# A state space layer's output scaling moved from VectorE to GpSimd, with two GpSimd operations written otherwise

## The chip, the cores and the metric

The kernel runs on one core of one Trainium2 chip, in one launch. The time is device microseconds of that core, from the first to the last instruction of a run; three runs were timed before the change. TensorE is called PE here, VectorE DVE, ScalarE ACT, GpSimd POOL and the sync engine, which issues the DMAs, SP.

## The reference, cut to what matters

A stack of eight layers works on x of shape (4, 32, 128, 128). The change touches one of them, the state space layer (`_mamba`), which runs over the 32 time steps of each of 4 x 128 sequences and whose result is normalised and added to x:

```python
xz = xt @ in_proj;  xc, z = xz[..., :D_INNER], xz[..., D_INNER:]
xc = silu(conv_b + sum_k conv_w[:, k] * shifted xc)        # D_INNER 256, 4 taps
dbc = xc @ x_proj
dt = softplus(dbc[..., :DT_RANK] @ dt_w + dt_b)
Bm, Cm = dbc[..., 8:24], dbc[..., 24:]                      # 16 states
dA = exp(dt[..., None] * A);  dBx = (dt * xc)[..., None] * Bm
hnew = dA_t * hprev + dBx_t;  y_t = einsum('bds,bs->bd', hnew, C_t)
y = (y + Dp * xc) * silu(z);  return y @ out_w + out_b
```

What follows the layer is h + that, then layernorm (x - mean) * rsqrt(var + 1e-5) * gain + shift, then + x.

## The kernel before

The layer is the function `mamba`. It works in 32 turns. One turn is 16 nodes of one batch entry with their 32 time steps: 512 tokens as columns (N), the 256 inner channels as two halves h of 128 partitions. A turn is cut into 16 units u. Each engine has its own program, written as a loop over slots `w` with `k, u = divmod(w, U)`; what it does in a slot, for which turn (k - 1, k, k + 1, k + 2, k + 3), is written out by `if u == ...` lines. So the engines' orders are fixed, and four turns are in flight. Semaphores alone hold the engines together; each engine takes its instructions strictly in order.

The loop of one turn k, as far as the prediction goes into it:

- PE: `project_x(k+2, h)` (L912) at u = 0 and 2 makes the channels, `flip` (L1018) turns two states' scan results every unit, `sums` (L1031) contracts them with C every second unit, `inputs` (L1004) makes the scan's input for the next two units, `project_out(k-1)` (L991) runs at u = 8.
- ACT: `x_in` (L1096) copies the channels into `xcp` at u = 0 and 2; `silu_x` (L1105) takes both convolved halves at u = 8, then `logarithms` (L1144), and in every unit `states_in` (L1170) copies the flipped states out of PSUM, which frees the bank for PE's next flip. The decays dA (L1162) of the next turn's first half run at u = 9 to 15, those of the second half at u = 0 to 4.
- POOL: `convolve(k+2, 0)` and `convolve(k+2, 1)` (L777, L779, L780: seven passes over 128 x 512 each) at u = 1 and 4. Between them stand `spread_c(k, 2)` (L816) and `gate(k-1, .)` (L823). `plus` (L788, L790) makes 1 + e at u = 15 and 0, `spread_b` (L808), `time_steps`, `bias` and `finish` (L838 to L840, gain, shift and + x) fill the rest; `deviations` (L832) gives rstd at u = 14.
- DVE: one scan (L1246, 128 x 1024) per unit, a copy of flipped states (L1256) every second unit, and at u = 5 and 7 `lost` (L1263, two inputs in SBUF), at u = 9, 11, 13 and 15 `residual`, `statistics`, `moments` and `scale(k-1)` (L1296).

A scan in the first unit of a turn waits for all 16 decays of its half, as `scan` says:

```python
dve.wait_ge(b_done, w // 2 + 1)
dve.wait_ge(dA_ready, (2 * i + h + 1) * S)
```

and the second silu of a turn waits for the second convolution, by `act.wait_ge(conv_ready, 2 * (i - EARLY) + h + 1)`.

The first turns' convolutions (0 and 1) are made on DVE ahead of the loop, so POOL convolves in turns k = 0 to 29.

Of the kernel before, what the change touches and what calls it, by code (L numbers as in the profile page):

```python
# [16 lines left out]
ALU = mybir.AluOpType  # L17
# [3 lines left out]
P = 128  # L21
B, T, W, C = 4, 32, 128, 128
# [581 lines left out]
def mamba(nc, h0, x, in_proj, conv_w, conv_b, x_proj, dt_w, dt_b, A_log, Dp, out_w, out_b, gain, shift,  # L604
# [7 lines left out]
    G, J = 4, 4  # L612
    NQ = W // Q
    N = Q * T
# [9 lines left out]
    S4 = S // 4  # L624
    with ExitStack() as ctx:
        s = Scope(nc, ctx, tag)
# [10 lines left out]
        ident = s.sb("ident", [P, P])  # L637
        m32 = s.sb("m32", [P, T])
        half_c = s.sb("half", [P, G])
        ht, hr, xt = (s.sb(n, [P, 2, G, C]) for n in ("ht", "hr", "xt"))  # L640
        hT = s.sb("hT", [P, N])
        xcp = s.sb("xcp", [P, HV, Q, PADT])
# [4 lines left out]
        e, ln = (s.sb(n, [P, HV, N]) for n in ("e", "ln"))  # L647
        bt, ct = s.sb("bt", [P, 2, G, S]), s.sb("ct", [P, 2, G, S])
        cp = s.sb("cp", [P, 2, J, G, S4])
        DB = s.sb("DB", [P, G, S, T])  # L650
        WC = s.sb("WC", [P, J, G, S4, T])
# [6 lines left out]
        z, out = s.sb("z", [P, G, C]), s.sb("out", [P, G, C])  # L658
        st, mv = s.sb("st", [P, G, 6]), s.sb("mv", [P, G, 2])
        ve, rstd = s.sb("ve", [P, G]), s.sb("rstd", [P, G])  # L660
# [25 lines left out]
        def turn(i):  # L686
            return 0 <= i < TURNS

        def unit(w):
            return 0 <= w < TURNS * U  # L690
# [62 lines left out]
        def _(pool):  # L753
            step = Chain(pool, pch)
            fill_identity(pool, step, ident)
            step(pool.memset(half_c[:, :], -0.5))
            step(pool.memset(xcp[:, :, :, 0:K - 1], 0.0))
            step(pool.memset(dA[:, :, :, :, 0:1], 0.0))
            step(pool.memset(m32[:, :], 0.0))
# [23 lines left out]
            def plus(i, h):  # L783
                pool.wait_ge(dt_read, 2 * i + h + 1)
                pool.wait_ge(e_ready, 2 * i + h + 1)
                if i >= 1:
                    pool.wait_ge(dt_ready, 2 * (i - 1) + h + 1)
                pool.tensor_tensor(dt[:, i % 2, h, :], dt[:, i % 2, h, :], e[:, h, :], ALU.add  # L788
                                   ).then_inc(plus_ready, 1)
                pool.tensor_scalar(ln[:, h, :], e[:, h, :], 1.0, None, ALU.add).then_inc(e1_ready, 1)  # L790

            def time_steps(i, h):
                pool.wait_ge(rest_ready, 2 * i + h + 1)
# [17 lines left out]
            def spread_c(i, g):  # L811
                pool.wait_ge(cp_ready, i + 1)
                if i >= 1:
                    pool.wait_ge(y_done, (i - 1) * V + G + g + 1)
                for j in range(J):
                    last = pool.tensor_tensor(  # L816
                        WC[:, j, g, :, :], cp[:, i % 2, j, g, :].unsqueeze(2).broadcast_to([P, S4, T]),
                        m32[:, :].unsqueeze(1).broadcast_to([P, S4, T]), ALU.mult)
                last.then_inc(WC_ready, 1)

            def gate(i, h):
                pool.wait_ge(y_taken, 2 * i + h + 1)
# [7 lines left out]
            def deviations(i):  # L830
                pool.wait_ge(ve_ready, i + 1)
                pool.tensor_tensor(rstd[:, :], ve[:, :], half_c[:, :], ALU.pow).then_inc(rstd_ready, 1)  # L832

            def finish(i):
                pool.wait_ge(scaled, i + 1)
# [6 lines left out]
            for w in SLOTS:  # L842
                k, u = divmod(w, U)
                if u == 0 and turn(k + 1):
                    plus(k + 1, 1)
                if u == 1:
                    if turn(k + 2) and k + 2 >= EARLY:
                        convolve(k + 2, 0)
                    if turn(k):
                        spread_c(k, 2)  # L850
                if u == 4:
                    if turn(k - 1):
                        gate(k - 1, 0)
                        gate(k - 1, 1)
                    if turn(k + 2) and k + 2 >= EARLY:
                        convolve(k + 2, 1)
                if u == 7:
                    if turn(k):
                        spread_c(k, 3)
                    if turn(k - 1):  # L860
                        bias(k - 1)
                if u in (9, 11, 13, 15) and turn(k + 1):
                    spread_b(k + 1, (u - 9) // 2)
                if u == 9 and turn(k + 1):
                    time_steps(k + 1, 0)
                    time_steps(k + 1, 1)
                if u == 11 and turn(k - 2):
                    finish(k - 2)
                if u == 14:
                    if turn(k + 1):  # L870
                        spread_c(k + 1, 0)
                    if turn(k - 1):
                        deviations(k - 1)
                if u == 15:
                    if turn(k + 2):
                        plus(k + 2, 0)
                    if turn(k + 1):
                        spread_c(k + 1, 1)
# [342 lines left out]
        def _(dve):  # L1221
            step = Chain(dve, dch)
            TT, TS, STT = dve.tensor_tensor, dve.tensor_scalar, dve.scalar_tensor_tensor
# [49 lines left out]
            def residual(i):  # L1273
                dve.wait_ge(outed, i + 1)
                dve.wait_ge(hr_ready, i + 1)
                TT(z[:, :, :], hr[:, i % 2, :, :], ps_0[:, :].rearrange("p (g c) -> p g c", g=G), ALU.add
                   ).then_inc(z_ready, 1)

# [5 lines left out]
            def moments(i):  # L1284
# [2 lines left out]
                    step.mark(dve.bn_aggr(mv[:, g, :], st[:, g, :]))  # L1287
                step.join()
                TS(ve[:, :], mv[:, :, 1], eps, None, ALU.add).then_inc(ve_ready, 1)

            def scale(i):
                dve.wait_ge(rstd_ready, i + 1)
                if i >= 1:
                    dve.wait_ge(stored, 16 * J * i)
                for g in range(G):
                    last = TS(out[:, g, :], z[:, g, :], mv[:, g, 0:1], rstd[:, g:g + 1],  # L1296
                              ALU.subtract, ALU.mult)
                last.then_inc(scaled, 1)

            for w in SLOTS:  # L1300
                k, u = divmod(w, U)
                if unit(w):
                    scan(w)
                if u % 2 == 1 and unit(w - 1):
                    states_in(w - 1)
                if u == 1 and turn(k - 1):
                    take_y(k - 1, 0)
                if k == -2 and u in (2, 4):
                    convolve(0, u // 2 - 1)
                if k == -2 and u in (10, 12):  # L1310
                    convolve(1, u // 2 - 5)
                if u == 3 and turn(k - 1):
                    take_y(k - 1, 1)
                if u in (5, 7) and turn(k + 1):
                    lost(k + 1, (u - 5) // 2)
                if u == 9 and turn(k - 1):
                    residual(k - 1)
                if u == 11 and turn(k - 1):
                    statistics(k - 1)
                if u == 13 and turn(k - 1):  # L1320
                    moments(k - 1)
                if u == 15 and turn(k - 1):
                    scale(k - 1)

# [3163 lines left out]
```

## Time and profile before

| what | value |
|---|---|
| median of three runs | 3863.41 us (3857.32 to 3867.41) |
| span of the profiled execution | 3864.4 us |
| busy share of the span: PE, DVE, ACT, POOL | 82%, 77%, 67%, 62% |
| largest group on DVE: L1246, the scan | 1141.5 us in 512 |
| L1296, the scaling on DVE | 128 instructions, median 332 ns |
| L816, the spread of C on POOL | 194.6 us in 512 |
| L790, 1 + e on POOL | 96.0 us in 64 |
| starts of the convolutions on POOL (L777), first and last | 497.6 and 1973.2 us |

The time of a run is that of the program on the core; the span of the profiled execution is the only time that the profile gives of it, and it stands 1.0 us above the median of the three runs. Read the shares with care: they are means over eight layers. The state space layer lies between about 440 and 2123 us, and the rows further down are taken from inside it. In a timeline row the first number is the start, the second how long the merged piece took, x4 means four instructions merged, and what stands in brackets is how long the engine was idle before it and what it waited for. Gaps of less than about 0.15 us are not shown as idle.

### The profile page before, as it was taken

To read this page: it belongs to the slowest core of one execution; us is meant where nothing else is said; L and a number is where in the kernel's file an instruction comes from. 1 tells how busy PE (TensorE), PEld (TensorE's weight loads), DVE (VectorE), ACT (ScalarE), POOL (GpSimd) and SP (SyncE) were. 2 spreads that over 40 slices of the span, in tenths; PEclk is the share of its full clock that TensorE was granted. 3 is DMA by queue.
4 is the path that set the end of the run, shared out by engine and by line. 5 is a ranking of instruction groups with operands and counts; after the bars stand their busy time and mean duration, and the time that the engine had idled before them with its cause. 6 is when DMAs were issued, how large, how long until landed. Compare 5 with 4: busy or idle time off the path is not lost. (4 is left out here: it accounts for less than half of the span.)

```text
span 3864.4 us, 82478 instructions
## 1 busy us (share of the span) xinstructions
PE 3158.9 (82%) x29152; PEld 2183.1 (56%) x29152; DVE 2993.7 (77%) x5896; ACT 2599.8 (67%) x5235; POOL 2377.3 (62%) x2879
## 2 busy tenths in 40 slices
PE   7999589999999999999986876688848856678486
PEld 3766356666666666666664563366636533456455
DVE  3999579999999999999997567389858663278754
ACT  4888489999999999999984210266756363077562
POOL 2899588898898999988874000177755130044850
PEclk7999799999999999999999568677769867789698
DMA  3000100000000000000000512501000014500424
GB/s 93 24 24 26 51 4 13 24 24 24 24 24 24 24 22 17 20 24 24 23 18 23 145 40 93 207 23 29 7 5 1 1 25 142 189 5 1 121 56 126
DMA packets 271007, 172.53 MB, mean 45 GB/s; under 512 B 41648, under 2 KB 249977, under 8 KB 268537
## 3 DMA queue, kind: packets, MB, share of 16 engines
q1 hardware_dynamic: 270600, 167.25, 15.1%
q8 instruction: 239, 3.92, 0.4%
q14 instruction: 168, 1.37, 0.1%
HBM read 116.59 MB, written 50.60 MB: 43 GB/s over the span
## 5 line engine op out<-in xcount | busy, mean ns | idle before, releaser
L1246 DVE TENSOR_TENSOR_SCAN mam_hs<-mam_dA,mam_ps_b 128x1024 f32<-128x1024 f32 x512 | 1141.5, 2270 | 80.9 <-issue 44.0
L1162 ACT ACTIVATE mam_dA<-mam_dt,mam_A 128x496 f32<-128x496 f32 x1024 | 658.7, 710 | 0.4
L1018 PE MATMUL mam_ps_h<-mam_ident,mam_hs 128*128 128x128 f32 x4096 | 549.6, 277 | 61.2 <-ACT mam_hTb L1170 30.8
L1018 PEld LDWEIGHTS mam_ps_h<-mam_ident,mam_hs 128*128 128x128 f32 x4096 | 454.0, 142 | 226.9 <-issue 149.2
L1170 ACT COPY mam_hTb<-mam_ps_h 128x512 f32<-128x512 f32 x768 | 424.5, 589 | 95.9 <-PE mam_ps_h L1018 95.9
L1004 PE MATMUL mam_ps_b<-mam_DB,mam_dtxt 32*128 32x512 f32 x2048 | 292.5, 638 | 77.6 <-DVE mam_hs L1246 73.6
L1031 PEld LDWEIGHTS mam_ps_y<-mam_hTb,mam_WC 128*32 128x32 f32 x8192 | 208.9, 109 | 133.2 <-issue 124.3
L1031 PE MATMUL mam_ps_y<-mam_hTb,mam_WC 128*32 128x128 f32 x8192 | 276.7, 275 | 0.3 <-issue 0.3
L780 POOL TENSOR_TENSOR mam_cv<-mam_cv,mam_tap 128x512 f32<-128x512 f32 x180 | 239.1, 1328 | 14.1
L816 POOL TENSOR_TENSOR mam_WC<-mam_cp,mam_m 128x128 f32<-128x128 f32 x512 | 194.6, 411 | 19.9 <-POOL mam_cv L780 14.8
L1256 DVE COPY mam_hTb<-mam_ps_h 128x512 f32<-128x512 f32 x256 | 174.3, 681 | 37.9 <-PE mam_ps_h L1018 35.9
L779 POOL TENSOR_TENSOR mam_tap<-mam_xcp,mam_cw 128x512 f32<-128x512 f32 x180 | 190.0, 1055 | 14.1
L460 ACT ACTIVATE gat_ex<-gat_ps_s,gat_neg 128x128 f32<-128x128 f32 x512 | 154.5, 436 | 50.6 <-DVE gat_neg L543 50.6
L2411 POOL TENSOR_TENSOR l1t_rs<-l1t_va,l1t_half 128x8 f32<-128x8 f32 x64 | 108.2, 1691 | 79.7 <-DVE l1t_va L2717 79.6
L1004 PEld LDWEIGHTS mam_ps_b<-mam_DB,mam_dtxt 32*128 32x128 f32 x2048 | 84.8, 183 | 127.9 <-issue 127.9
L256 POOL TENSOR_TENSOR gat_ex<-gat_ex,gat_den 128x512 f32<-128x512 f32 x128 | 133.0, 1050 | 36.3 <-DVE gat_den L552 36.3
L808 POOL TENSOR_TENSOR mam_DB<-mam_bt,mam_m 128x512 f32<-128x512 f32 x128 | 134.2, 1049 | 17.8 <-PE mam_ps_b L1004 17.8
L945 PE MATMUL mam_ps<-mam_xs,mam_wdt 128*128 128x512 f32 x248 | 118.4, 600 | 1.9 <-issue 1.9
L3744 POOL MEMSET sma_half<- 128x4 f32 x1 | 0.1, 103 | 184.5 <-POOLq L82 184.5
L788 POOL TENSOR_TENSOR mam_dt<-mam_dt,mam_e 128x512 f32<-128x512 f32 x64 | 81.8, 1279 | 43.3 <-ACT mam_e L1139 26.8
L543 DVE TENSOR_REDUCE gat_neg<-gat_ps_s 128x4 f32<-128x512 f32 x128 | 81.6, 679 | 22.2 <-PE gat_ps_s L343 22.2
L790 POOL TENSOR_SCALAR mam_ln<-mam_e 128x512 f32<-128x512 f32 x64 | 96.0, 1501 | 0.0
(738 smaller groups left out, 8290.4 us busy)
## 6 DMA issues: line engine op xcount, KB each, us to landing
moe_wg<-in_L_ffn_weight SPq DMA_DIRECT2D x32, 1024.0 KB, 8.2
rnn_xr<-x SPq DMA_DIRECT2D x23, 512.0 KB, 5.7
l1y_wh<-mode_weights SPq DMA_DIRECT2D x16, 544.0 KB, 3.7
gat_hg<-in_x SPq DMA_DIRECT2D x16, 512.0 KB, 7.1
h<-gat_out SPq DMA_DIRECT2D x32, 256.0 KB, 2.3
mam_ht<-h SPq DMA_DIRECT2D x128, 64.0 KB, 2.0
mam_hr<-h SPq DMA_DIRECT2D x128, 64.0 KB, 2.0
mam_xt<-in_x SPq DMA_DIRECT2D x128, 64.0 KB, 2.0
```

What stands on the lines that cost most here:

```text
L460: last = act.activation(ex[:, i % 2, h, r, :], ps_s[h][:, r * W:(r + 1) * W], ACT.Exp, bias=neg[:, i % 2, h, r:r + 1])
L779: step(pool.tensor_tensor(tap[:, :, :], xcp[:, h, :, k:k + T], weight(k), ALU.mult))
L780: step(pool.tensor_tensor(acc, acc, tap[:, :, :], ALU.add))
L808: pool.tensor_tensor(DB[:, g, :, :], bt[:, i % 2, g, :].unsqueeze(2).broadcast_to([P, S, T]), m32[:, :].unsqueeze(1).broadcast_to([P, S, T ...
L816: last = pool.tensor_tensor(WC[:, j, g, :, :], cp[:, i % 2, j, g, :].unsqueeze(2).broadcast_to([P, S4, T]), m32[:, :].unsqueeze(1).broadca ...
L1004: last = pe.matmul(ps_b[:, j, :], steps[r, g * P:(g + 1) * P], DB[r, g, :, :].rearrange("p s t -> p (s t)"), start=True, stop=True, tile_p ...
L1018: last = pe.transpose(ps_h[n][:, q * P:(q + 1) * P], hs[:, w % 3, c:c + P], ident[:, :])
L1031: last = pe.matmul(ps_y[j * T:(j + 1) * T, g * P:(g + 1) * P], WC[:, j, g, q, :], hTb[:, gg % 2, j, q, :], start=(q == 0), stop=(q == S4 - 1),
L1162: act.activation(dA[:, h, :, n, 1:], dt[:, i % 2, h, :].rearrange("p (q t) -> p q t", q=Q)[:, :, 1:], ACT.Exp, scale=A[:, h, n:n + 1]).the ...
L1170: act.copy(hTb[:, gg % 2, j, :, :], ps_h[n][:, :].rearrange("p (q d) -> p q d", q=S4)).then_inc(hB_ready if n else hA_ready, 1)
L1246: dve.tensor_tensor_scan(hs[:, w % 3, :], dA[:, h, first:first + 2, :, :].rearrange("p q s t -> p (q s t)"), ps_b[:, 2 * (w % 2):2 * (w % ...
L1256: dve.tensor_copy(hTb[:, gg % 2, 2 * (w % 2) + 1, :, :], ps_h[1][:, :].rearrange("p (q d) -> p q d", q=S4)).then_inc(hB_ready, 1)
```

## The change

Three things change, all in `mamba`. First, `scale` leaves DVE (u = 15 of the turn that follows) and is done on POOL at u = 3 of the turn after that, between `spread_c(k, 2)` and `gate(k-1, 0)`; `residual` on DVE, which writes z anew, now waits until the previous turn's z was scaled. Second, `spread_c` writes the four blocks j of a group in one instruction of 128 x 4 x 128 in place of four of 128 x 128. Third, 1 + e is a tensor_tensor with a column of ones, broadcast, in place of a tensor_scalar with the constant 1.

```diff
+        one_c = s.sb("one", [P, 1])
...
             step(pool.memset(half_c[:, :], -0.5))
+            step(pool.memset(one_c[:, :], 1.0))
...
-                pool.tensor_scalar(ln[:, h, :], e[:, h, :], 1.0, None, ALU.add).then_inc(e1_ready, 1)
+                pool.tensor_tensor(ln[:, h, :], e[:, h, :], one_c[:, :].broadcast_to([P, N]), ALU.add
+                                   ).then_inc(e1_ready, 1)
...
-                for j in range(J):
-                    last = pool.tensor_tensor(
-                        WC[:, j, g, :, :], cp[:, i % 2, j, g, :].unsqueeze(2).broadcast_to([P, S4, T]),
-                        m32[:, :].unsqueeze(1).broadcast_to([P, S4, T]), ALU.mult)
-                last.then_inc(WC_ready, 1)
+                every = [P, J, S4, T]
+                pool.tensor_tensor(WC[:, :, g, :, :], cp[:, i % 2, :, g, :].unsqueeze(3).broadcast_to(every),
+                                   m32[:, :].unsqueeze(1).unsqueeze(1).broadcast_to(every), ALU.mult).then_inc(WC_ready, 1)
...
+            def scale(i):
+                pool.wait_ge(rstd_ready, i + 1)
+                if i >= 1:
+                    pool.wait_ge(stored, 16 * J * i)
+                for g in range(G):
+                    last = pool.tensor_scalar(out[:, g, :], z[:, g, :], mv[:, g, 0:1], rstd[:, g:g + 1],
+                                              ALU.subtract, ALU.mult)
+                last.then_inc(scaled, 1)
...
+                if u == 3 and turn(k - 2):
+                    scale(k - 2)
...
             def residual(i):
                 dve.wait_ge(outed, i + 1)
                 dve.wait_ge(hr_ready, i + 1)
+                if i >= 1:
+                    dve.wait_ge(scaled, i)
...
-            def scale(i):
-                dve.wait_ge(rstd_ready, i + 1)
-                if i >= 1:
-                    dve.wait_ge(stored, 16 * J * i)
-                for g in range(G):
-                    last = TS(out[:, g, :], z[:, g, :], mv[:, g, 0:1], rstd[:, g:g + 1],
-                              ALU.subtract, ALU.mult)
-                last.then_inc(scaled, 1)
...
-                if u == 15 and turn(k - 1):
-                    scale(k - 1)
```

POOL's order in the middle of a turn, from the last two passes of the first convolution (names: cv and tap are the convolution's sum and product, WC the spread C, y the gated output). Before:

```order
L779 TENSOR_TENSOR mam_tap<-mam_xcp,mam_cw 128x512
L780 TENSOR_TENSOR mam_cv<-mam_cv,mam_tap 128x512
L816 TENSOR_TENSOR mam_WC<-mam_cp,mam_m 128x128 x4
L823 TENSOR_TENSOR mam_y<-mam_y,mam_sz 128x512 x2
L777 TENSOR_TENSOR mam_cv<-mam_xcp,mam_cw 128x512
```

and of the change:

```order
L781 TENSOR_TENSOR mam_tap<-mam_xcp,mam_cw 128x512
L782 TENSOR_TENSOR mam_cv<-mam_cv,mam_tap 128x512
L819 TENSOR_TENSOR mam_WC<-mam_cp,mam_m 128x4x128
L840 TENSOR_SCALAR mam_out<-mam_z,mam_mv,mam_rstd 128x128 x4
L824 TENSOR_TENSOR mam_y<-mam_y,mam_sz 128x512 x2
L779 TENSOR_TENSOR mam_cv<-mam_xcp,mam_cw 128x512
```

The four scalings now stand between the two convolutions; the lines are numbered two or more higher.

DVE's order at the end of a turn (hs is the scan's result, mv and ve mean and variance; the scan is printed as SCALAR_TENSOR_TENSOR here). Before:

```order
L1289 TENSOR_SCALAR mam_ve<-mam_mv 128x4
L1246 SCALAR_TENSOR_TENSOR mam_hs<-mam_dA,mam_ps_b 128x1024 x2
L1256 COPY mam_hTb<-mam_ps_h 128x512
L1296 TENSOR_SCALAR mam_out<-mam_z,mam_mv,mam_rstd 128x128 x4
L1246 SCALAR_TENSOR_TENSOR mam_hs<-mam_dA,mam_ps_b 128x1024 x2
```

and of the change:

```order
L1303 TENSOR_SCALAR mam_ve<-mam_mv 128x4
L1258 SCALAR_TENSOR_TENSOR mam_hs<-mam_dA,mam_ps_b 128x1024 x2
L1268 COPY mam_hTb<-mam_ps_h 128x512
L1258 SCALAR_TENSOR_TENSOR mam_hs<-mam_dA,mam_ps_b 128x1024 x2
```

The four scalings ahead of the next turn's first scan are gone. PE, ACT and SP keep their orders.

## Rows read from the trace of the kernel before

**Rows 1.** Stretches, 608 to 2000 us: busy us (x instructions) of PE, PEld, DVE, ACT, POOL; clock, DMA.

```profile
608.00:2000.00 1392.00, 1281.09 (x15148) 875.08 (x15148) 1311.44 (x1160) 1279.00 (x2234) 1254.28 (x1354) 1.00 0.09 22
```

**Rows 2.** Timeline of DVE, a turn's boundary: start us, us, instruction, [idle before <-releaser].

```profile
1249.23 1.19 DVE L1296 TENSOR_SCALAR mam_out<-mam_z,mam_mv,mam_rstd 128x128 f32<-128x128 f32 x4
1251.91 4.46 DVE L1246 TENSOR_TENSOR_SCAN mam_hs<-mam_dA,mam_ps_b 128x1024 f32<-128x1024 f32 x2 [1.49 <-issue]
```

**Rows 3.** Timeline of ACT, the same boundary.

```profile
1250.49 1.33 ACT L1162 ACTIVATE mam_dA<-mam_dt,mam_A 128x496 f32<-128x496 f32 x2
```

**Rows 4.** Timeline of ACT, the silu of two halves, in three turns.

```profile
519.10 1.33 ACT L1105 ACTIVATE mam_xs<-mam_cv,mam_cb 128x512 f32<-128x512 f32 x2
...
1203.18 0.59 ACT L1096 COPY mam_xcp<-mam_ps 128x512 f32<-128x512 f32 x1 [0.30 <-PE mam_ps L912]
...
1224.73 1.41 ACT L1105 ACTIVATE mam_xs<-mam_cv,mam_cb 128x512 f32<-128x512 f32 x2
...
1228.51 1.06 ACT L1170 COPY mam_hTb<-mam_ps_h 128x512 f32<-128x512 f32 x2
...
1780.44 0.72 ACT L1105 ACTIVATE mam_xs<-mam_cv,mam_cb 128x512 f32<-128x512 f32 x1 [0.27 <-POOLq L781]
```

**Rows 5.** Timeline of POOL, u = 0 to 8 of one turn.

```profile
1201.14 1.49 POOL L790 TENSOR_SCALAR mam_ln<-mam_e 128x512 f32<-128x512 f32 x1
1203.86 1.05 POOL L777 TENSOR_TENSOR mam_cv<-mam_xcp,mam_cw 128x512 f32<-128x512 f32 x1 [1.23 <-ACT mam_xcp L1096]
...
1212.61 1.47 POOL L816 TENSOR_TENSOR mam_WC<-mam_cp,mam_m 128x128 f32<-128x128 f32 x4 [0.24 <-POOL mam_cv L780]
...
1216.51 1.04 POOL L777 TENSOR_TENSOR mam_cv<-mam_xcp,mam_cw 128x512 f32<-128x512 f32 x1
...
1218.76 1.60 POOL L780 TENSOR_TENSOR mam_cv<-mam_cv,mam_tap 128x512 f32<-128x512 f32 x1
...
1224.07 1.27 POOL L780 TENSOR_TENSOR mam_cv<-mam_cv,mam_tap 128x512 f32<-128x512 f32 x1
```

**Rows 6.** Timeline of PE, the same turn.

```profile
1202.05 1.10 PE L912 MATMUL mam_ps<-mam_hT,mam_w_in 128*128 128x512 f32 x2
...
1227.15 1.95 PE L991 MATMUL mam_ps<-mam_ow,mam_y 128*128 128x128 f32 x16
1229.22 1.07 PE L1018 MATMUL mam_ps_h<-mam_ident,mam_hs 128*128 128x128 f32 x8
1230.40 1.14 PE L1004 MATMUL mam_ps_b<-mam_DB,mam_dtxt 32*128 32x512 f32 x8
...
1252.44 1.10 PE L912 MATMUL mam_ps<-mam_hT,mam_w_in 128*128 128x512 f32 x2
```

**Rows 7.** Timeline of POOL, the one turn with a longer gap.

```profile
1758.58 1.05 POOL L777 TENSOR_TENSOR mam_cv<-mam_xcp,mam_cw 128x512 f32<-128x512 f32 x1 [1.23 <-ACT mam_xcp L1096]
...
1767.62 1.48 POOL L816 TENSOR_TENSOR mam_WC<-mam_cp,mam_m 128x128 f32<-128x128 f32 x4 [0.53 <-POOL mam_cv L780]
...
1809.27 1.06 POOL L777 TENSOR_TENSOR mam_cv<-mam_xcp,mam_cw 128x512 f32<-128x512 f32 x1 [1.23 <-ACT mam_xcp L1096]
```

**Rows 8.** Groups of POOL (L808) and timeline of POOL in the last stage (L4228).

```profile
L808 POOL TENSOR_TENSOR mam_DB<-mam_bt,mam_m 128x512 f32<-128x512 f32 x128 | 134.2, 1049 | 17.8 <-PE mam_ps_b L1004 17.8
...
3690.89 1.32 POOL L4228 TENSOR_SCALAR rnna_u<-rnn_xr,rnna_rs,rnna_nb 128x128 f32<-128x128 f32 x3
```

**Rows 9.** Timeline of DVE, L1263 alone and twice beside POOL.

```profile
512.37 0.68 DVE L1263 SCALAR_TENSOR_TENSOR mam_e<-mam_ln,mam_dt 128x512 f32<-128x512 f32 x1
...
1218.10 1.13 DVE L1263 SCALAR_TENSOR_TENSOR mam_e<-mam_ln,mam_dt 128x512 f32<-128x512 f32 x1
...
1224.21 1.68 DVE L1263 SCALAR_TENSOR_TENSOR mam_e<-mam_ln,mam_dt 128x512 f32<-128x512 f32 x1
```

**Rows 10.** DMA issues of the stores: KB each, us to landing.

```profile
x<-mam_out SPq DMA_DIRECT2D x128, 64.0 KB, 1.8
```

**Rows 11.** Timeline of DVE, the last turn's scaling.

```profile
2116.25 1.11 DVE L1296 TENSOR_SCALAR mam_out<-mam_z,mam_mv,mam_rstd 128x128 f32<-128x128 f32 x4 [2.36 <-DMA x<-mam_out]
```

## The prediction

> **What bounds the kernel now.** I read the stretches first, then the boundary between two turns on DVE and ACT, then one whole turn on POOL, ACT and PE. In the steady part of the layer all four engines are busy between 90% and 94% of the time, at full granted clock [rows 1]. DVE is the busiest, which says only that no engine is far from being the bound. Which one is must be read from who waits last.
>
> At the end of a turn DVE does the four scalings, 1249.23 to 1250.42, and then idles 1.49 us before the next turn's first scan at 1251.91 [rows 2]. The idle is marked "issue", so the profile names no releaser, but that scan waits for all 16 decays of its half, and ACT ends the last two of them at 1250.49 + 1.33 = 1251.82 [rows 3], 0.09 us ahead of it. The scalings lie wholly inside a wait for ACT. Their removal makes that wait longer and starts no scan sooner.
>
> What sets the turn, 50.39 us from one PE pass L912 to the next [rows 6], is a loop through POOL. PE's L912 at 1202.05 is copied by ACT (1203.18 to 1203.77) [rows 4]; POOL, which had idled 1.23 us for that copy, starts the first convolution at 1203.86 and ends the second at 1224.07 + 1.27 = 1225.34 [rows 5]. ACT's second silu needs it. Two silus in a row that wait for nothing take 1.33 us (519.10); in this turn they take 1.41 [rows 4], so the second started 0.08 us late, at about 1225.42, which is 0.08 after POOL's end: it waits for POOL. It is so in 24 of the 25 turns after 560 us that I placed this way: the second silu starts 0.08 to 0.10 us after POOL's end. Behind it ACT loads a table, takes two logarithms and then the copy of flipped states at 1228.51 [rows 4], which ends at 1229.10; PE, whose pass L991 also ends at 1229.10, starts its next flip at 1229.22 [rows 6] and shows no idle longer than 0.11 us from there to L912 of the next turn at 1252.44. Sum: 1.81 (PE, ACT) + 21.48 (POOL) + 3.88 (ACT) + 23.22 (PE) = 50.39.
>
> The trace holds a natural trial of this. In one turn POOL's gap ahead of L816 was 0.53 us in place of 0.24 [rows 7, 5]; ACT then idled a visible 0.27 us for POOL [rows 4], and the next turn's first convolution came 1809.27 - 1758.58 = 50.69 us after this one's, about 0.3 us more than the usual 50.4. A delay between the two convolutions goes into the turn one for one.
>
> **The change part by part.** Only what lies on POOL between 1203.86 and 1225.34 counts fully.
>
> *Spread of C, turn's third group.* Four instructions took 1.47 us [rows 5]. One of 512 columns with both inputs broadcast, as L808 is, takes 1.05 [rows 8]. Gain 0.42 us. The output of the new one is in four pieces; if that makes it as slow as a pass with two full inputs (1.27, rows 5), the gain is 0.20. The other three groups of a turn lie behind the second convolution, where POOL's later idle times hold what they save: nothing.
>
> *1 + e.* L790 takes 1.49 us [rows 5], a pass with one broadcast operand 1.05 (L777, same rows). It saves 0.44 twice a turn, ahead of the 1.23 us for which POOL waits for ACT: the wait grows, gain nothing. If the new form were slower, up to 1.23 us would be hidden just the same.
>
> *Scaling on POOL.* The nearest rows are L4228, the same form (128 x 128, two columns of scalars): three in 1.32 us with a mean of 0.45, so a pitch of 0.43 [rows 8]. Four cost 1.73 us. Bounds: DVE's own 0.33 for each below (1.19 for four with overlaps, rows 2), and 0.48 above: a quarter of L790's 1.49 is 0.37, and a pass over 128 columns costs 0.11 more than a quarter of one over 512, as L816 (a quarter of 1.47) does against L808 (a quarter of 1.05) [rows 5, 8]. I take 0.43, the nearest form. Waits: rstd was made by POOL itself in the turn before; the stores behind `stored` land 1.8 us after their issue [rows 10] and were issued some eight units, half a turn, earlier. Neither holds POOL, hence neither holds the gate and the convolution queued behind. DVE's new wait ahead of `residual` is for POOL's work of six units earlier, some 19 us; it costs nothing as long as POOL is not that late, and the scans behind it are not held.
>
> *A collision moved.* L1263 on DVE (two inputs in SBUF) takes 0.68 us when nothing is in its way, and 1.13 and 1.68 in a usual turn [rows 9]. Both fit one picture: it stands still until POOL's pass under way ends (1218.68 and 1225.34), then needs 0.55 more, while POOL's next reading pass waits. L780 at 1218.76 shows the other side, 1.60 in place of 1.27 [rows 5]: 0.33 us. The second collision now costs the convolution nothing, since its last pass, at 1224.07, is the one that DVE waits for. With POOL 1.31 us later (1.73 - 0.42), DVE's second L1263 comes at about 1224.4 while two passes are still to run, and the last of them is held another 0.32 us. The Trainium skill, "SBUF — State Buffer", section "Who interferes with whom", has the same as a rule: a DVE instruction with two SBUF inputs and a GpSimd instruction that reads SBUF exclude each other for the whole instruction, and whoever starts first keeps the ports. The rows agree.
>
> So POOL ends the second convolution 1.73 - 0.42 + 0.32 = 1.63 us later. One thing gives a little back: PE's L1004 at 1230.40 stands 0.11 us behind the flip's end at 1230.29 [rows 6], held by a scan that ends on DVE at that time; with PE later, that gap closes. Net 1.52 us a turn.
>
> Scaling and convolution stand together in turns 2 to 29, 28 turns: 42.6 us. At the end of the layer the last scaling waits 2.36 us for a store, then takes 1.11 on DVE [rows 11]; on POOL it takes some 0.6 longer, less a hop between engines: 0.5. The other layers are untouched. **Sum: 3864.4 + 43.1 = 3907.5 against the profiled execution, which stands 1.0 above the median; for the median 3906.**
>
> A page would put one term lower. The Trainium skill, "GPSIMD Engine Reference", section "Engine selection", tells not to put elementwise work on GpSimd, and gives about twice DVE's time for two inputs, but nearly line rate for one. The rows speak against the second half: L790 with one input (1.49) is slower on POOL than passes with two (1.05 and 1.27). What it would give stands as a rival below.
>
> **The rivals.**
> - *The scalings cost on POOL what they cost on DVE.* One-input passes run at DVE's speed: four take 1.19 [rows 2], 0.54 less than in my sum, so 0.98 a turn, 28 x 0.98 + 0.5 = 28: 3891. Against it stands L4228, the same form. This is the page's rule.
> - *DVE is the bound after all.* It is the busiest [rows 1]. If the 1.49 us ahead of the first scan were a cost that follows the scalings and not a wait for ACT, the scan would start 1.19 us sooner in 32 turns: 3863 - 38 = 3825. It decides if scans follow the end of DVE's own work; the 0.09 us between ACT's last decay and the scan [rows 2, 3] speak against it, and so does the silu's wait for POOL, which would have to vanish too.
> - *POOL's order does not matter, only its sum.* Per turn POOL saves 4 x 0.42 + 2 x 0.44 = 2.56 and gains 1.73, so it is less busy than before. If ACT could take other work while the convolution is late, or its 0.32 us waits further on absorbed the delay, the time would stay: 3863. ACT takes its instructions in order, and the late turn of rows 7 absorbed nothing.
> - *Only the collision stays away* (DVE shifts too): 28 x 1.20 + 0.5 = 34: 3897.
>
> **How the numbers follow.** Forecast 3906 with its near variants (slower spread, dearer scaling, up to 28 x (0.22 + 0.20) = 12 us more, 3918; no collision, 3897): 0.74. Scaling at DVE's price, 3891: 0.11. DVE the bound, 3825: 0.07. Nothing moves: 0.08, of which 0.06 within 0.3% and 0.02 on the fast side. A difference under 0.3%, 11.6 us, could not be told from none. Slower by more than that: 0.85; same 0.06; faster 0.09. The range reaches from 3884 (DVE's price and no collision, 28 x 0.66 + 0.5 = 19 more, less the scatter of the median) up to 3922; it leaves out the last two cases, 0.15, and 0.05 of the others' tails.
>
> **What the profile would show.** Right: turns of about 51.9 us from one L912 to the next; four scalings at a pitch of 0.43 on POOL between C's spread (1.05) and the gate; a visible idle on ACT of about 1.6 us ahead of the second silu, named POOL; PE idle some 1.5 us ahead of the flip after L991; the wait ahead of a turn's first scan on DVE longer, about 2.7 us. Wrong: turns of 50.4 us or less, silus that still follow each other at once, or a first scan that follows DVE's copy at once. A wait on `residual` would show a missed cost, and one-pass spreads over 1.3 us a misjudged one.

## The result, and the profile after

| | before | the change |
|---|---|---|
| median | 3862.01 us (3857.32 to 3867.41, 4 runs) | 3978.19 us (3974.84 to 3983.43, 4 runs) |
| ratio | | 1.0306, 95% interval 1.0292 to 1.032 |
| profiled span | 3864.4 us | 3973.1 us |
| one turn, from one first convolution on POOL to the next | 50.4 us | 54.7 to 54.9 us in 24 turns, 53.3 in 3, 50.2 and 50.8 in the first two |

The change costs 116 us. The direction was as forecast, the size was not: 43 us had been forecast, and 3978 lies outside the range. The 29 distances between first convolutions add up to 1462.9 us before and 1575.3 after, 112.4 us more; the layer as a whole, from its first POOL instruction to the next layer's, grew by 119.6 (1690.4 to 1810.0), the rest lying in the turns behind the last of these distances. The two profiled spans differ by only 108.7, because the layers outside took 11 us less in the changed kernel's profile; they scatter by that much from profile to profile. In the experiments below one run of twelve of the kernel with the two rewrites alone took 11194 us; its median counts that run, its ratio does not.

The stretch of [rows 1] in the changed kernel; the clock, the first number behind PE's, DVE's, ACT's and POOL's busy times, is no longer 1.00:

```profile
608.00:2000.00 1392.00, 1219.97 (x13969) 822.66 (x13970) 1213.35 (x975) 1188.24 (x2062) 1171.93 (x1045) 0.97 0.08 21
```

The end of a turn on DVE, as [rows 2]; start, duration, what, idle before:

```profile
1294.43 0.69 DVE L1268 COPY mam_hTb<-mam_ps_h 128x512 f32<-128x512 f32 x1 [0.73 <-PE mam_ps_h L1030]
1297.71 4.46 DVE L1258 TENSOR_TENSOR_SCAN mam_hs<-mam_dA,mam_ps_b 128x1024 f32<-128x1024 f32 x2 [2.59 <-ACT mam_dA L1174]
```

ACT in the same turn, as [rows 3, 4]. The last row holds the last two decays:

```profile
1266.53 0.72 ACT L1117 ACTIVATE mam_xs<-mam_cv,mam_cb 128x512 f32<-128x512 f32 x1
1269.86 0.72 ACT L1117 ACTIVATE mam_xs<-mam_cv,mam_cb 128x512 f32<-128x512 f32 x1 [2.61 <-POOLq L783]
...
1272.95 1.06 ACT L1182 COPY mam_hTb<-mam_ps_h 128x512 f32<-128x512 f32 x2
...
1296.29 1.33 ACT L1174 ACTIVATE mam_dA<-mam_dt,mam_A 128x496 f32<-128x496 f32 x2
```

The scalings are gone from DVE, and the wait grew from 1.49 to 2.59 us. The scan starts at 1297.71, 0.09 us after ACT's last decay (1296.29 + 1.33 = 1297.62), just as before. Freeing DVE bought nothing here. The second silu now waits a visible 2.61 us for POOL.

POOL in that turn, as [rows 5]:

```profile
1245.30 1.05 POOL L779 TENSOR_TENSOR mam_cv<-mam_xcp,mam_cw 128x512 f32<-128x512 f32 x1 [1.69 <-ACT mam_xcp L1108]
...
1254.05 1.05 POOL L819 TENSOR_TENSOR mam_WC<-mam_cp,mam_m 128x512 f32<-128x512 f32 x1 [0.24 <-POOL mam_cv L782]
1255.08 3.13 POOL L840 TENSOR_SCALAR mam_out<-mam_z,mam_mv,mam_rstd 128x128 f32<-128x128 f32 x4
1258.18 2.50 POOL L824 TENSOR_TENSOR mam_y<-mam_y,mam_sz 128x512 f32<-128x512 f32 x2
...
1261.76 1.39 POOL L781 TENSOR_TENSOR mam_tap<-mam_xcp,mam_cw 128x512 f32<-128x512 f32 x1
...
1268.18 1.60 POOL L782 TENSOR_TENSOR mam_cv<-mam_cv,mam_tap 128x512 f32<-128x512 f32 x1
...
1297.32 1.03 POOL L792 TENSOR_TENSOR mam_ln<-mam_e,mam_one 128x512 f32<-128x512 f32 x1
```

C's spread takes 1.05 us, 1 + e 1.03, both as priced. The four scalings take 3.13 us in place of the 1.73 that I had put. Both collisions with DVE's L1263 (L1275 now) lie inside the second convolution, on L781 (1.39 for 1.05) and on the last L782 (1.60 for 1.27). The stretch from 1245.30 to 1268.18 + 1.60 = 1269.78 is 24.48 us, 3.00 more than before.

PE, as [rows 6]:

```profile
1243.50 1.10 PE L924 MATMUL mam_ps<-mam_hT,mam_w_in 128*128 128x512 f32 x2
...
1269.76 1.95 PE L1003 MATMUL mam_ps<-mam_ow,mam_y 128*128 128x128 f32 x16
1273.66 1.16 PE L1030 MATMUL mam_ps_h<-mam_ident,mam_hs 128*128 128x128 f32 x8 [1.95 <-ACT mam_hTb L1182]
1274.75 2.09 PE L1016 MATMUL mam_ps_b<-mam_DB,mam_dtxt 32*128 32x512 f32 x8
1276.77 1.61 PE L1043 MATMUL mam_ps_y<-mam_hTb,mam_WC 128*32 128x128 f32 x32
...
1298.24 1.10 PE L924 MATMUL mam_ps<-mam_hT,mam_w_in 128*128 128x512 f32 x2
```

L924 to L924 is 54.74 us. PE idles 1.95 us ahead of the flip at 1273.66. Then comes what no row of before had: `inputs` (L1016) takes 2.09 us in place of 1.14, `sums` (L1043) 1.61 in place of the 1.08 of before:

```profile
1231.47 1.08 PE L1031 MATMUL mam_ps_y<-mam_hTb,mam_WC 128*32 128x128 f32 x32
```

Around that moment the windows of the changed kernel show the granted clock (the number after POOL's busy time and count):

```profile
1270.00:1274.00 4.00, 2.05 (x19) 1.89 (x18) 3.02 (x2) 3.97 (x6) 3.98 (x4) 1.00 0.00 0
1274.00:1275.00 1.00, 1.00 (x11) 0.72 (x13) 0.14 (x1) 0.66 (x3) 0.92 (x2) 0.75 0.00 0
1275.00:1276.00 1.00, 1.00 (x8) 0.27 (x8) 1.00 (x2) 1.00 (x1) 1.00 (x2) 0.50 0.00 0
1276.00:1277.00 1.00, 1.00 (x11) 0.21 (x10) 0.23 (x2) 0.99 (x3) 1.00 (x1) 0.50 0.00 0
1277.00:1278.00 1.00, 1.00 (x28) 0.94 (x23) 1.00 (x1) 0.53 (x1) 0.92 (x2) 0.55 0.00 0
1278.00:1279.00 1.00, 1.00 (x22) 0.80 (x12) 1.00 (x1) 0.54 (x1) 1.00 (x2) 1.00 0.00 0
```

PE's clock falls from 1.00 (2.4 GHz) to 0.50 (1.2 GHz) within a microsecond of the end of the idle, and comes back some 3 us later. This costs the turn 54.74 - 53.3 = 1.4 us, in 24 of the 27 measured turns that have scaling and convolution together. The three turns of 53.3 have the same idle and keep the full clock, as this one, in which `inputs` takes its 1.14:

```profile
1110.82 1.07 PE L1030 MATMUL mam_ps_h<-mam_ident,mam_hs 128*128 128x128 f32 x8 [1.95 <-ACT mam_hTb L1182]
1111.81 1.14 PE L1016 MATMUL mam_ps_b<-mam_DB,mam_dtxt 32*128 32x512 f32 x8
```

So the idle of 1.95 us alone does not decide whether the clock falls. PE has shorter idles too in the 30 us ahead of it, of 0.35 to 0.90 us each.

### The profile page after: what moved, and what is told of

Read it like the earlier page. It is cut to its first block and busy times, and to the rows that moved or that the text cites. A ratio compares the mean times of both kernels' runs of the same rounds, so it can differ in the third digit from the quotient of the medians.

```text
span 3973.1 us, 82063 instructions
## 1 busy us (share of the span) xinstructions
PE 3182.9 (80%) x29120; PEld 2188.0 (55%) x29152; DVE 2992.8 (75%) x5768; ACT 2608.0 (66%) x5235; POOL 2392.8 (60%) x2624
## 5 line engine op out<-in xcount | busy, mean ns | idle before, releaser
L1030 PE MATMUL mam_ps_h<-mam_ident,mam_hs 128*128 128x128 f32 x4096 | 560.0, 280 | 122.2 <-ACT mam_hTb L1182 85.8
L1016 PE MATMUL mam_ps_b<-mam_DB,mam_dtxt 32*128 32x512 f32 x2048 | 314.6, 684 | 94.3 <-DVE mam_hs L1258 93.2
L1043 PEld LDWEIGHTS mam_ps_y<-mam_hTb,mam_WC 128*32 128x32 f32 x8192 | 214.8, 112 | 151.5 <-issue 137.9
L1043 PE MATMUL mam_ps_y<-mam_hTb,mam_WC 128*32 128x128 f32 x8192 | 283.7, 280 | 0.3 <-issue 0.3
L782 POOL TENSOR_TENSOR mam_cv<-mam_cv,mam_tap 128x512 f32<-128x512 f32 x180 | 237.5, 1320 | 14.1
L781 POOL TENSOR_TENSOR mam_tap<-mam_xcp,mam_cw 128x512 f32<-128x512 f32 x180 | 199.3, 1107 | 14.1
L1016 PEld LDWEIGHTS mam_ps_b<-mam_DB,mam_dtxt 32*128 32x128 f32 x2048 | 89.6, 194 | 147.2 <-issue 147.2
L819 POOL TENSOR_TENSOR mam_WC<-mam_cp,mam_m 128x512 f32<-128x512 f32 x128 | 134.4, 1050 | 25.2 <-POOL mam_cv L782 14.2
L1275 DVE SCALAR_TENSOR_TENSOR mam_e<-mam_ln,mam_dt 128x512 f32<-128x512 f32 x64 | 124.4, 1944 | 7.3 <-POOL mam_ln L792 7.3
L833 POOL TENSOR_TENSOR mam_rstd<-mam_ve,mam_half 128x4 f32<-128x4 f32 x32 | 32.9, 1029 | 127.5 <-DVE mam_ve L1303 127.5
```

The source lines that it names most:

```text
L781: step(pool.tensor_tensor(tap[:, :, :], xcp[:, h, :, k:k + T], weight(k), ALU.mult))
L782: step(pool.tensor_tensor(acc, acc, tap[:, :, :], ALU.add))
L819: pool.tensor_tensor(WC[:, :, g, :, :], cp[:, i % 2, :, g, :].unsqueeze(3).broadcast_to(every), m32[:, :].unsqueeze(1).unsqueeze(1).broadc ...
L1016: last = pe.matmul(ps_b[:, j, :], steps[r, g * P:(g + 1) * P], DB[r, g, :, :].rearrange("p s t -> p (s t)"), start=True, stop=True, tile_p ...
L1030: last = pe.transpose(ps_h[n][:, q * P:(q + 1) * P], hs[:, w % 3, c:c + P], ident[:, :])
L1043: last = pe.matmul(ps_y[j * T:(j + 1) * T, g * P:(g + 1) * P], WC[:, j, g, q, :], hTb[:, gg % 2, j, q, :], start=(q == 0), stop=(q == S4 - 1),
```

## The experiments

Each ratio is to the kernel before, timed on the same chip. Turn lengths are distances between the first convolutions of successive turns on POOL. Where turns are given for a kernel with more work or the scaling on POOL, the first one or two, which have none of it yet, are left out.

**The two rewrites alone.** The scaling goes back to DVE at u = 15; spread of C and 1 + e stay as changed.

```diff
-                if u == 3 and turn(k - 2):
-                    scale(k - 2)
...
+                if u == 15 and turn(k - 1):
+                    scale(k - 1)
```

> The change without its first part: the scaling stays on DVE at u = 15, the spread of C is one pass and 1 + e adds the broadcast column. Theory (a POOL loop with PE 0.1 us behind): the second convolution ends 0.42 us sooner, the second silu follows the first at once (1.33 us for the pair), and PE's own chain takes over after 0.1 us; turns of 50.3 us in place of 50.4, 3 us in all, so 3859 to 3862, no difference that can be told. Rival (POOL's time is the bound): 0.42 us a turn is kept, 30 turns, 12 us faster. Rival (one of the two rewrites is itself part of the loss): slower than before by 3 us or more, the L816 successor over 1.3 us or the successor of L790 over 1.5.

Measured: 3857.9 us, ratio 0.9983 (0.997 to 0.9996), turns of 50.23 us. POOL and ACT there:

```profile
1221.23 1.27 POOL L782 TENSOR_TENSOR mam_cv<-mam_cv,mam_tap 128x512 f32<-128x512 f32 x1
1222.74 1.22 POOL L819 TENSOR_TENSOR mam_WC<-mam_cp,mam_m 128x512 f32<-128x512 f32 x1 [0.24 <-POOL mam_cv L782]
```

```profile
1222.30 1.34 ACT L1106 ACTIVATE mam_xs<-mam_cv,mam_cb 128x512 f32<-128x512 f32 x2
```

The second convolution ends at 1222.50 and the two silus run at once (1.34 us for the pair, the second starting near 1222.9). POOL no longer holds up the second silu; the turn became 0.19 us shorter, not 0.42 and not 0.1. Whatever binds next is 0.19 us behind POOL's loop. The rewrites are no part of the loss.

**The scaling alone.** The kernel before with the scaling on POOL at u = 3.

```diff
+                if u == 3 and turn(k - 2):
+                    scale(k - 2)
...
-                if u == 15 and turn(k - 1):
-                    scale(k - 1)
```

> The kernel before with the scaling alone moved to POOL at u = 3; spread of C in four passes and 1 + e as before. Theory: all of the loss is the scaling's. The scalings take 0.79 us each as in the changed kernel, the second convolution ends 3.1 + 0.3 us later than before, 0.42 later than in the changed kernel; turns of 55.1 to 55.2 us, total 3978 + 28 x 0.42 = 3990 us. Rival (the rewrites cost something): 3978 or less.

Measured: 3990.98 us, ratio 1.0321. Its turns have two lengths, 53.72 to 53.75 (12 turns) and 55.15 to 55.29 (15 turns): each 0.42 above the change's 53.3 and 54.75, as expected of the four-pass spread, but with the lower clock in 15 turns in place of 24, which I had not expected: PE's idle ahead of the flip is 1.92 to 1.95 us in all 27, with and without a fall. The turns' sum is the change's (1574.5 against 1575.3): nine falls fewer give back what the four-pass spread costs. The layer takes 1811.8 us against 1810.0 in the change; nearly all of the 25 us between the two profiled spans lie in other layers (436.3 us ahead of this one against 426.6, 1749.9 behind it against 1736.5). So all of the loss is the scaling's, while the agreement of the total with the expected 3990 is luck.

**Four forms of the scaling in one kernel.** Each of the four groups gets its own pair of operations, all else as in the change.

```diff
-                for g in range(G):
-                    last = pool.tensor_scalar(out[:, g, :], z[:, g, :], mv[:, g, 0:1], rstd[:, g:g + 1],
-                                              ALU.subtract, ALU.mult)
+                pool.tensor_scalar(out[:, 0, :], z[:, 0, :], mv[:, 0, 0:1], rstd[:, 0:1], ALU.add, ALU.mult)
+                pool.tensor_scalar(out[:, 1, :], z[:, 1, :], mv[:, 1, 0:1], rstd[:, 1:2], ALU.mult, ALU.add)
+                pool.tensor_scalar(out[:, 2, :], z[:, 2, :], mv[:, 2, 0:1], rstd[:, 2:3], ALU.subtract, ALU.subtract)
+                pool.tensor_scalar(out[:, 3, :], z[:, 3, :], 0.25, 0.5, ALU.subtract, ALU.mult).then_inc(scaled, 1)
```

> The changed kernel with another pair of operations in each of the four scalings, on a line of its own: add and mult with columns; mult and add with columns (the form of the last layer's 0.45 us); subtract twice with columns; subtract and mult with two constants. It leaves the normalisation wrong in all four groups; all else is computed. Theory 1 (the pair of operations sets the price): mult and add takes 0.45, the others 0.79 or in between. Theory 2 (the place: DVE scans meanwhile, or the layout of z, mean and rstd): all with columns take 0.79, the one with constants may be less. Theory 3 (the columns): the one with constants takes about 0.4, the others 0.79.

Measured in a single run: 3958.25 us, 20 of the 27 turns 53.96 to 54.12 us long, seven 52.60 to 52.65. The groups of this kernel, count, busy us and mean ns:

```profile
L841 POOL TENSOR_SCALAR mam_out<-mam_z,mam_mv,mam_rstd 128x128 f32<-128x128 f32 x32 | 25.8, 807 | 0.0
...
L842 POOL TENSOR_SCALAR mam_out<-mam_z 128x128 f32<-128x128 f32 x32 | 20.8, 651 | 0.0
...
L840 POOL TENSOR_SCALAR mam_out<-mam_z,mam_mv,mam_rstd 128x128 f32<-128x128 f32 x32 | 14.5, 453 | 0.0
L839 POOL TENSOR_SCALAR mam_out<-mam_z,mam_mv,mam_rstd 128x128 f32<-128x128 f32 x32 | 14.5, 452 | 2.2 <-DMA x<-mam_out 2.1
```

and the change's own row for subtract and mult, shortest, median and longest of 128:

```profile
L840 POOL TENSOR_SCALAR mam_out<-mam_z,mam_mv,mam_rstd x128: 787/793/802, 600.9 to 2226.4; 128x128 f32<-128x128 f32 x128
```

Add and mult 452 ns, mult and add 453, subtract and mult 793, subtract twice 807; subtract and mult with two constants 651. All stand at the same place in the turn, on the same tiles and with the same strides. The pairs that begin with a subtract are the dear ones: the pair of operations sets the price, as theory 1 says, though it had put only mult and add at 0.45. Other pairs were not tried. Constants in place of columns save 0.14 of it.

**Mult and add in all four.**

```diff
-                                              ALU.subtract, ALU.mult)
+                                              ALU.mult, ALU.add)
```

> The changed kernel with mult and add in place of subtract and mult in the scaling on POOL; it computes z * mean + rstd in place of the normalised value, all else is as in the changed kernel. Theory (the pair of operations sets the price): scalings at a pitch of 0.43, the second convolution ends 1.6 us later than before, turns of 51.9 us, PE's granted clock stays at 2.4 GHz, 3905 us, as the prediction said. If the price stays at 0.79: 3978 us. If the price falls but PE's clock still drops for some microseconds of each turn: 3905 plus up to 28 x 1.45 = 3945 us.

Measured: 3915.48 us, ratio 1.0129 (1.0108 to 1.0149). 22 of the 27 turns are 51.89 to 51.98 us long, five 53.35 to 53.43. The scalings:

```profile
L840 POOL TENSOR_SCALAR mam_out<-mam_z,mam_mv,mam_rstd 128x128 f32<-128x128 f32 x128 | 55.6, 448 | 1.3 <-DMA x<-mam_out 1.2
```

With the price that the prediction had used, the turn is the one that it had worked out (51.9), and the layer's loss 49.7 us (1740.1 against 1690.4), 43 forecast and five turns with a dropped clock (7 us). 3915 lies inside the range of the prediction. PE's idle ahead of the flip is 1.69 to 1.75 us here.

**PE kept at work.** The change, with 12 of the 16 matmuls of the output projection made twice, ahead of the idle.

```diff
+                for g in range(G - 1):
+                    cols = slice(g * P, (g + 1) * P)
+                    for h in range(HV):
+                        last = pe.matmul(ps_0[:, cols], y[:, h, cols], ow[:, h, :],
+                                         start=(h == 0), stop=(h == HV - 1))
                 last.then_inc(outed, 1)
```

> The changed kernel in which PE makes 12 of the 16 matmuls of the output projection (L1003, three of four groups, 1.46 us) a second time, just where PE then waits 1.95 us for ACT; the results are the same. Theory (of the 4.3 us that a turn grew, 2.87 are POOL's and about 1.45 come of PE's clock dropping to 1.2 GHz after its idle): the idle shrinks to about 0.5 us, the clock stays at 2.4 GHz, turns of 53.3 us in place of 54.7, 3978 - 27 x 1.45 = 3939 us, although PE does more work. Rival (the second matmuls' cost is simply hidden and the long inputs pass is contention of another kind): 3978. Rival (more work on a busy PE): slower than 3978.

Measured: 3958.23 us, ratio 1.0236 (1.0218 to 1.0255). All 27 turns are 53.30 to 53.34 us long. PE in one of them, and the windows there:

```profile
1265.41 1.95 PE L1003 MATMUL mam_ps<-mam_ow,mam_y 128*128 128x128 f32 x16
1267.20 1.50 PE L1008 MATMUL mam_ps<-mam_ow,mam_y 128*128 128x128 f32 x12
1269.31 1.06 PE L1035 MATMUL mam_ps_h<-mam_ident,mam_hs 128*128 128x128 f32 x8 [0.61 <-ACT mam_hTb L1187]
1270.31 1.14 PE L1021 MATMUL mam_ps_b<-mam_DB,mam_dtxt 32*128 32x512 f32 x8
```

```profile
1266.00:1270.00 4.00, 3.39 (x32) 3.22 (x31) 2.67 (x2) 3.65 (x7) 4.00 (x4) 1.00 0.00 0
1270.00:1274.00 4.00, 4.00 (x59) 2.88 (x58) 3.59 (x4) 3.97 (x6) 3.84 (x4) 1.00 0.03 6
```

The idle is 0.61 us, the clock stays at 1.00, `inputs` takes its 1.14 again. More work on PE made the kernel 20 us faster than the change. In the layer the gain is 32.8 us (1777.2 against 1810.0): 24 falls at 1.45 are 34.8, less 1.2 for the turn ahead of the first scaling, which the repeated matmuls made longer (51.46 against 50.24), and 0.6 in the last turns. The whole gained less, since the other layers took longer in this kernel's profile (437.5 against 426.6 us ahead, 1747.1 against 1736.5 behind), which I can't explain and which is of the size by which they scatter from kernel to kernel. With PE kept at work the clock falls in no turn, so the long passes are the clock's, not a contention. The run does not tell whether the length of this one idle counts or PE's work around it as a whole.

**One POOL pass more, two POOL passes more.** The kernel before, the first tap's product in the second convolution made once again (the first dose) or twice again (the second). The edit of the first; the second has 2 in place of the first 1.

```diff
+                    for _ in range(1 if h == 1 and k == 1 else 0):
+                        step(pool.tensor_tensor(tap[:, :, :], xcp[:, h, :, k:k + T], weight(k), ALU.mult))
```

> The kernel before with one pass more on POOL inside the second convolution (the first tap's product made twice, 1.05 us and 0.08 to the next), same results. Theory (POOL's stretch from the copy to the second silu is the loop; PE 0.1 to 0.2 us behind): turns longer by 1.13 and at most 0.33 more from the collision with L1263, less 0.2: 51.4 to 51.8 us, 30 turns, 3892 to 3903; PE's clock stays mostly at 2.4 GHz. Rival (something else is the loop): turns of 50.4 us, 3863.

> As the run with one pass more, but with two: 2.26 us more on POOL. Theory: turns of 52.5 to 52.8 us at a full clock, 3930 to 3936; where PE's idle ahead of the flip after the output projection is followed by a drop of the clock, 1.45 more for those turns, up to 3975. So more than twice the loss of the first dose if the clock drops, twice or a little more if it does not.

Measured: one pass 3904.35 us, ratio 1.0105 (1.0087 to 1.0123), turns of 51.76 to 51.84; two passes 3978.24, ratio 1.03 (1.0281 to 1.0318), four turns of 52.90 to 52.95 and 24 of 54.3 to 54.7. The sums hold to 0.04 us: 50.43 + 1.13 + 0.33 (a second collision) - 0.11 (PE's gap closed) = 51.78, and 1.13 more is 52.91. The first pass costs 41 us, the second 74 more: not the same again, but the same with the clock's fall. PE's idle ahead of the flip is about 1.6 us with one pass more, where none of the 28 turns has a fall, and about 2.7 with two:

```profile
1226.44 1.06 PE L1020 MATMUL mam_ps_h<-mam_ident,mam_hs 128*128 128x128 f32 x8 [2.73 <-ACT mam_hTb L1172]
1227.43 2.09 PE L1006 MATMUL mam_ps_b<-mam_DB,mam_dtxt 32*128 32x512 f32 x8
```

An idle of 2.73 us, then `inputs` at 2.09. A kernel whose DVE program is untouched loses as much as the change does, from delay on POOL alone.

**The scaling where POOL idles, as add and mult.** DVE makes minus the mean (one instruction on 128 x 4), POOL scales at u = 0, ahead of the first convolution.

```diff
+                step(TS(nm[:, :], mv[:, :, 0], -1.0, None, ALU.mult))
...
-                    last = pool.tensor_scalar(out[:, g, :], z[:, g, :], mv[:, g, 0:1], rstd[:, g:g + 1],
-                                              ALU.subtract, ALU.mult)
+                    last = pool.tensor_scalar(out[:, g, :], z[:, g, :], nm[:, g:g + 1], rstd[:, g:g + 1],
+                                              ALU.add, ALU.mult)
...
-                if u == 3 and turn(k - 2):
+                if u == 0 and turn(k - 2):
                     scale(k - 2)
```

> The changed kernel with the scaling as add and mult (DVE makes minus the mean, one small instruction a turn) and put on POOL at u = 0, behind 1 + e and ahead of the first convolution, where POOL idles 1.69 us for ACT's copy. Theory: four scalings at a pitch of 0.43 are 1.73 us, all but 0.04 in that idle; turns as without the scaling on POOL, 50.2 to 50.3 us, 3855 to 3862. DVE is 1.2 us emptier a turn and nothing comes of it. Rival (DVE is a bound too): clearly below 3855. Rival (POOL is late at the first convolution nevertheless): 3870 or more.

Measured: 3856.06 us, ratio 0.9979 (0.9967 to 0.999), turns of 50.23.

```profile
1241.39 1.03 POOL L793 TENSOR_TENSOR mam_ln<-mam_e,mam_one 128x512 f32<-128x512 f32 x1
1242.42 1.74 POOL L841 TENSOR_SCALAR mam_out<-mam_z,mam_nm,mam_rstd 128x128 f32<-128x128 f32 x4
1244.13 1.05 POOL L780 TENSOR_TENSOR mam_cv<-mam_xcp,mam_cw 128x512 f32<-128x512 f32 x1
```

The four take 1.74 us and fill POOL's idle; the convolution follows at once. The turn is that of the two rewrites alone: an emptier DVE is worth nothing there, and the filled idle on POOL costs nothing. Against the run with mult and add, whose four scalings cost the same (1.8 us) but stand at u = 3, it is the place on POOL that makes the difference, 3856 against 3915 us.

**A copy moved from ACT to DVE, with the scaling on POOL and with it on DVE.**

```diff
-                    if u % 2 == 0:
+                    if u % 2 == 0 and u != 14:
                         states_in(w - 1, 1)
...
-                if u % 2 == 1 and unit(w - 1):
+                if (u % 2 == 1 or u == 14) and unit(w - 1):
                     states_in(w - 1)
```

> The kernel with the scaling on POOL at u = 0 as add and mult, and besides one copy of flipped states (the second one at u = 14) moved from ACT to DVE, which the moved scaling has made 1.2 us emptier. Theory (a turn of 50.23 us is bound by the loop DVE scan, PE, ACT, PE, ACT decays, with POOL's convolution stretch 0.2 us behind it): ACT's last decays come 0.47 us sooner, the first scan of a turn too, and turns shrink by 0.2 us until POOL's stretch binds again: 50.0 to 50.1 us, 3850. Rival (the 50.23 us are PE's own unbroken stretch): 50.23, 3856. Rival (the copy on DVE delays the scan of u = 15 and with it PE's flips): longer turns, 3865 or more.

> The same copy moved to DVE, but with the scaling left on DVE (otherwise the kernel with the two rewrites alone). Theory: before its first scan DVE still waits for ACT by 1.49 - 0.47 - 0.6, about 0.4 us, so there is room for both and the turn is as with the scaling on POOL: 50.0 to 50.1 us, 3850 to 3852. If DVE's room is what the scaling's place buys: slower than that run by 0.2 us a turn or more, 3857 or more.

Measured: with the scaling on POOL 3855.22 us, ratio 0.9975 (0.9961 to 0.999), turns of 50.09 to 50.15; with it on DVE 3866.51, ratio 1.0001 (0.9986 to 1.0015), turns of 50.44 to 50.49. The first gained 0.11 of the 0.2 us expected and can't be told from the run without the moved copy by its total; its turns tell it. The second lost 0.22 us a turn where I expected room. What took the room stands on DVE and POOL:

```profile
1241.91 2.81 DVE L1297 TENSOR_SCALAR mam_out<-mam_z,mam_mv,mam_rstd 128x128 f32<-128x128 f32 x4
1244.64 4.45 DVE L1247 TENSOR_TENSOR_SCAN mam_hs<-mam_dA,mam_ps_b 128x1024 f32<-128x1024 f32 x2
```

```profile
1242.28 1.36 POOL L790 TENSOR_TENSOR mam_dt<-mam_dt,mam_e 128x512 f32<-128x512 f32 x1 [0.91 <-ACT mam_dt L1138]
1243.60 1.03 POOL L792 TENSOR_TENSOR mam_ln<-mam_e,mam_one 128x512 f32<-128x512 f32 x1
```

Four scalings on DVE took 2.81 us, from 1241.91, where two passes of POOL run. They take 1.11 when nothing is in their way [rows 11], and in the kernel with the two rewrites alone, where they start in POOL's idle:

```profile
1246.67 1.11 DVE L1297 TENSOR_SCALAR mam_out<-mam_z,mam_mv,mam_rstd 128x128 f32<-128x128 f32 x4
```

With the copy moved they had slid from POOL's idle onto its passes for dt and 1 + e, and the scan behind them came at 1244.64, though ACT had ended its last decays at 1243.83. With the scaling on POOL there is no such instruction on DVE.

## Why the prediction was right and wrong

- *The bound.* Right. The turn is a loop through POOL's stretch from ACT's copy to the second silu. One pass more in it lengthens the turn by its own length and the collision, less PE's closed gap of 0.11 us; leaving DVE alone or freeing it changes nothing. Only with ACT's copy moved to DVE besides does the scaling's place on DVE count, 0.33 us a turn (50.12 against 50.45).
- *The removal from DVE worth nothing.* Right, by [rows 2, 3] and the 2.59 us of after. "DVE is the bound after all" is refuted by the changed trace and the scaling at u = 0, "POOL's order does not matter" by four scalings of 1.8 us in all that cost some 53 us at u = 3 and nothing at u = 0.
- *Spread of C, 1 + e, collision.* Right: 1.05, 1.03, and a second 0.33 us inside the convolution.
- *Scaling on POOL.* Here the prediction failed: this term was mis-sized. It called L4228 "the same form" and took 0.43 us, with 0.48 as the upper bound. L4228 is the same instruction on the same shape with columns as scalars, but with mult and add, where the scaling has subtract and mult. That pair costs 0.79: 3.10 us a turn in place of 1.73, 28 x 1.37 = 38 us. The upper bound was drawn from a pass with add, so it did not bound a subtract. The rival "the scalings cost on POOL what they cost on DVE" went the wrong way altogether. The Trainium skill, "GPSIMD Engine Reference", section "Engine selection", has one-input work on GpSimd at about line rate; the scaling took 793 ns on POOL against 332 on DVE, which disagrees, and the measurement decides. With the cheap pair in its place the kernel took 3915 us, inside the range.
- *PE's clock.* No term was made for it. "PE idle some 1.5 us ahead of the flip" was foreseen and its consequence was not: 24 turns x 1.45 = 35 us. The dear scalings brought most of it: with the price that was forecast the clock fell in 5 turns of 27 only, as the run with mult and add shows (7 us).
- *The sum.* 43 + 38 + 35 = 116, against 116 measured. So close an agreement is partly luck: in the profiles the layer alone grew by 119.6 us, and the other layers took less. The price alone, 3906 + 38 = 3944, leaves the range; the clock's falls came on top.
- *The range.* Its lower end, 3884, does not follow from its own 19 us, which give 3882. Nothing hangs on it.

## What to carry to other kernels

Where four engines are all above 90% busy, find the loop by times that agree to a tenth: a pair of silus that takes 0.08 us longer than it does elsewhere was the sign of who waits for whom. Work moved off the busiest engine onto one that lies on that loop costs its full length, at the new engine's price for exactly that pair of operations; look for a row with the same operations, not only the same shape, or write the operation as the cheap pair (add of a negated mean). The same work costs nothing where that engine idles: 1.74 us of scaling fitted into POOL's wait for ACT. And when a change lets TensorE idle about 2 us in every turn, price the passes behind it at the lower clock for a part of the turns, and say that the part is open.

## What the runs showed of the hardware

- POOL, tensor_scalar, 128 x 128 f32, two columns as scalars: 452 ns (add, mult), 453 (mult, add), 793 (subtract, mult), 807 (subtract, subtract); 651 with constants (subtract, mult).
- POOL, 128 x 512 f32: adding a constant by tensor_scalar took 1.49 us, adding a broadcast column of ones by tensor_tensor 1.03. Four passes of 128 x 128 with broadcast inputs took 1.47 us, one of 128 x 4 x 128 took 1.05.
- PE's granted clock fell from 1.00 to 0.50 for some 3 us, right behind PE's idle ahead of the flip, in this part of the turns: 24 of 27 in the change (idle 1.95 us), 15 of 27 with the scaling alone (the same 1.95), 24 of 28 with two passes more (2.7), 5 of 27 with mult and add (1.7), none of 28 with one pass more (1.6), none of 27 with the idle cut to 0.61 by repeated matmuls. Why some turns fall and others, with the same idle, don't is open. The price in this loop is 1.4 us a fall. The Trainium skill, "TensorE: Matmul & The Clock Gate", section "Part 1: The HAM clock gate", says that the clock is set to 1.2 or 2.4 GHz by how busy TensorE has been; the traces agree, and so does the run with repeated matmuls, where more work kept it at 2.4.
- Four tensor_scalar on DVE from SBUF to SBUF took 2.81 us beside POOL passes and 1.11 without: they are held up, as L1263 with its two SBUF inputs is. The Trainium skill, "SBUF — State Buffer", section "Who interferes with whom", counts tensor_scalar among the operations that can take the ports which DVE shares with GpSimd; the trace agrees.
